# Second layer's dense pass reordered, its queries and values loaded sooner, and the first attention's keys queued behind its queries

## The chip, the cores and the metric

The kernel runs on one core of one Trainium2 chip. The metric is the device time of one execution in microseconds; the median of three runs is 2421.66 (2420.82 to 2422.63). The engines are TensorE (PE; weight loads PEld), VectorE (DVE), ScalarE (ACT), GpSimd (POOL) and SyncE (SP), which here only issues DMAs.

## What is computed

Two transformer layers with a layer norm behind each part, on 2048 tokens of width 512, in float32:

```
x = layernorm(x + causal_attention(x))        # 16 heads of 32, rotary on half of each head
x = layernorm(x + experts(x))                 # 8 experts, top 2, and a shared one
x = layernorm(x + attention(x))               # one head of 512, q and k with bias and rotary
x = layernorm(x + gated_mlp(x, 2 of 4 kept))
```

Second layer's attention: `q = rope((x Wq + bq) * scale)`, `k = rope(x Wk + bk)`, `v = x Wv + bv`, `softmax(q kT) v Wo`. Rotary: `[x1, x2] -> [x1 cos - x2 sin, x2 cos + x1 sin]` with x1 and x2 the halves of a head of 128.

## The kernel before

Each engine has a program of its own, written out in order; semaphores order the engines among each other. Every product is made of three passes (`mm3`): each operand is split into a high part (ACT's copy to a reduced type) and a low part (DVE subtracts the high part).

**First attention** (`layer0_attention`). The work is cut into 16 items n = (chunk c of 512 queries, group g of 4 heads). A planner (`attention0_plan`) writes one list `order`, that PE, ACT, DVE and POOL all follow: "unit" (a block of scores for the row maxima), "turn" (maxima transposed), "scores", "av", "den". SP loads queries into 3 slots and keys into 8 slots (an item of chunk c uses c + 1 slots) and stores and reloads the row of maxima ("m": store, wait, load). Its list `work` is sorted by a place in `order`: the place at which the slot comes free, or at which the turn three items before stands (`soon`). A load of queries or keys is three DMAs of 256 KB (L528 keys, L534 queries). PE waits at the first unit of an item for its queries, then for its keys (L705 is the units' matmul, L726 and L731 that of the scores).

**Second layer's dense pass** (`layer1_attention`). Four chunks c of 512 tokens, four tiles k of 128 in each. Four pairs p of pieces in a chunk: queries 0 and 1, keys 0 and 1, keys 2 and 3, queries 2 and 3. PE makes for a chunk eight pieces i of 512 x 512 (`piece`, a ring of four banks `qk`: piece i waits for ACT's and DVE's reading of piece i-4), transposes (`turn`, L1844) and values (`value`) of tiles. For a pair p:

- ACT `out(i)` (L1557) copies a piece with its bias to `qkf`; DVE `turning` (L1711) makes bias and sine product `across`; POOL `cosines` (L1486) multiplies both halves of `qkf` with the cosines in one instruction of 1024.
- DVE (L1716, L1717) subtracts and adds: `turned`. ACT `high` (L1571) makes the high half, DVE `low` (L1726) the low half. For queries SP stores both to `q_dram` (L1437), keys stay in SBUF.

Beside it the tiles of the next chunk are prepared: POOL gathers two rows of experts' results per token (`gather`), DVE adds them to X and takes statistics (`stats`, L1678 to L791), ACT `root`, DVE `apply` (L1690, L1692), ACT `apply` (L1537) norm the tile; PE transposes it (tile k waits for DVE's `turn` of tile k-2), ACT and DVE `turn` (L1546, L1698) split it to `xch`, `xcl`. Values: ACT and DVE `value` (L1579, L1730) write `vhl`, of two buffers, SP `v_out` (L1426) stores it; ACT's `value(k)` waits until the store of tile k-2 has landed. SP's order in a chunk: the queries of pairs 0 and 3, the next chunk's tables `cs`, then four value tiles.

Behind the pass tile n = 0 of the attention has its scores already (`scores(0, b)` with `qf`); PE then runs `scores(n + 1, b)` (needs `load(n + 1)`, L1422) between the transposes of tile n (L1932), and the A·V product of tile n. The values are read back from `v_dram` as eight loads of 1 MB (L1461), high and low for each chunk; A·V of tile 0 waits for them quarter by quarter (`vload`). DVE `peak(0)`, ACT `exps(0)` (L1586) stand between scores and transposes.

## Time and profile before

| | |
|---|---|
| median of three runs | 2421.66 us |
| the profiled execution's own time | 2422.3 us |
| its span | 2420.5 us |
| PE busy | 2215.2 us, 92% |
| DVE, ACT, POOL busy | 1212.9, 746.1, 640.3 us |
| first attention | about 165 to 790 us |
| second layer's dense pass | about 1280 to 1462 us |
| second layer's attention behind it, then MLP | from 1475 us |

All times of rows are of one execution, in us from the start of its span; "ns" is written where meant. A timeline row says when an instruction started and how long it took; [x <- y] says how long the engine stood idle before it and whose semaphore ended that. PEclk is the clock that TensorE was granted, 1.00 for 2.4 GHz and 0.50 for 1.2 GHz.

### The profile page before, as it was taken

How to read it: one execution, taken by the hardware profiler on the slowest of the kernel's cores; microseconds unless marked ns; L12 is line 12 of the kernel's file. 1: busy time of each engine (PE TensorE's matmuls, PEld its weight loads, DVE VectorE, ACT ScalarE, POOL GpSimd, SP SyncE). 2: the span in 40 equal slices, each digit the busy share in tenths (PEclk: the TensorE clock that was granted, in tenths of full speed). 3: DMA queues.
4: the chain of work that ended last, by engine and by line, in shares of the span. 5: the costliest groups of instructions: out<-in, count | busy, mean ns of one | idle time of the engine just before them, and what ended most of it. 6: DMA issues, size and time to landing. Idle time of an engine off the chain costs nothing. (4 is left out here: it accounts for less than half of the span.)

```text
span 2420.5 us, 27398 instructions
## 1 busy us (share of the span) xinstructions
PE 2215.2 (92%) x10140; PEld 1521.5 (63%) x10140; DVE 1212.9 (50%) x2272; ACT 746.1 (31%) x1334; POOL 640.3 (26%) x434
## 2 busy tenths in 40 slices
PE   7977999999999679999988887999999999999996
PEld 5854555555553444444446776888887787878775
DVE  6864577776661543222237662322325555455656
ACT  3322455555556332111124331111113221121222
POOL 4342455564556105010023433000003021211200
PEclk9976799999999889999999998999999999999998
DMA  4564244443210524132234435000001010100001
GB/s 172 179 179 123 80 114 124 109 97 79 66 27 19 174 97 174 61 118 79 79 118 131 148 105 200 27 23 21 27 27 53 1 35 18 35 17 17 18 18 52
DMA packets 102058, 196.07 MB, mean 81 GB/s; under 512 B 10080, under 2 KB 27360, under 8 KB 100512
## 3 DMA queue, kind: packets, MB, share of 16 engines
q1 hardware_dynamic: 92832, 164.29, 22.6%
q0 software_dynamic: 8240, 27.01, 3.3%
q10 hardware_dynamic: 864, 3.15, 0.4%
q8 instruction: 77, 1.26, 0.2%
q14 instruction: 45, 0.37, 0.1%
HBM read 127.69 MB, written 66.72 MB: 80 GB/s over the span
## 5 line engine op out<-in xcount | busy, mean ns | idle before, releaser
L619 ACT ACTIVATE a_probs<-a_stb 128x512 f32<-128x512 f32 (+3 forms) x640 | 308.8, 535 | 283.4 <-PE a_stb L731 168.3
L590 POOL TENSOR_TENSOR a_probs<-a_probs 128x1024 f32<-128x1024 f32 (+3 forms) x160 | 281.5, 1773 | 289.6 <-PE a_avb L743 274.6
L645 DVE TENSOR_REDUCE a_mparts<-a_sbank 128x1 f32<-128x512 f32 x384 | 239.6, 683 | 100.0 <-PE a_sbank L705 99.8
L2049 POOL CAST m_wh<-wst 128x1024 fp32r<-128x1024 f32 x24 | 27.8, 1157 | 732.6 <-POOLq L1367 377.0
L56 PE MATMUL m_gu<-hi,m_wh 128*128 128x512 f32 x512 | 202.9, 396 | 14.5 <-DVE m_h L2115 13.1
L58 PE MATMUL m_gu<-hi,m_wl 128*128 128x512 f32 x512 | 202.0, 395 | 0.0
L57 PE MATMUL m_gu<-lo,m_wh 128*128 128x512 f32 x512 | 201.9, 394 | 0.0
L743 PE MATMUL a_avb<-a_probs,V 128*32 128x512 f32 (+3 forms) x1280 | 155.3, 558 | 0.7 <-ACT a_probs L619 0.7
L650 DVE CUSTOM_DVE_ANT_0 a_junk<-a_sbank,hidden 128x128 bf16<-128x128 f32 (+3 forms) x256 | 113.6, 488 | 83.5 <-PE a_sbank L705 81.7
L705 PE MATMUL a_sbank<-hi,q 96*128 96x512 f32 (+3 forms) x320 | 133.6, 447 | 23.7 <-PEq L152 12.1
L2115 DVE TENSOR_TENSOR m_h<-m_sg,m_gu 128x512 f32<-128x512 f32 x64 | 43.9, 686 | 208.5 <-ACT m_sg L2079 208.4
L705 PE MATMUL a_sbank<-lo,q 96*128 96x512 f32 (+3 forms) x320 | 120.0, 411 | 17.5 <-DMA q<-qk 11.1
L726 PE MATMUL a_stb<-q,hi 97*128 97x512 f32 (+3 forms) x320 | 133.1, 427 | 1.6 <-ACT a_probs L619 1.5
L1810 DVE TENSOR_TENSOR ptl<-q_tb,pth 128x512 fp32r<-128x512 f32 x64 | 44.1, 691 | 157.5 <-ACT pth L1661 157.5
L2079 ACT ACTIVATE m_sg<-m_gu 128x512 f32<-128x512 f32 x64 | 38.3, 598 | 273.2 <-PE m_gu L58 250.1
L726 PE MATMUL a_stb<-q,lo 97*128 97x512 f32 (+3 forms) x320 | 120.6, 389 | 1.6 <-ACT a_probs L619 1.1
L56 PEld LDWEIGHTS m_gu<-hi,m_wh 128*128 128x128 f32 x512 | 97.8, 191 | 37.8 <-DVE m_h L2115 15.6
L1661 ACT ACTIVATE pth<-q_tb 128x512 fp32r<-128x512 f32 x64 | 38.2, 598 | 254.5 <-PE q_tb L1932 254.5
L56 PE MATMUL q_qk<-hi,q 128*128 128x512 f32 x240 | 98.6, 411 | 13.4 <-DMA q<-q 13.4
L58 PEld LDWEIGHTS m_gu<-hi,m_wl 128*128 128x128 f32 x512 | 97.7, 191 | 20.6
L57 PEld LDWEIGHTS m_gu<-lo,m_wh 128*128 128x128 f32 x512 | 97.7, 191 | 20.4
L726 PEld LDWEIGHTS a_stb<-q,hi 97*128 97x128 f32 x320 | 62.6, 198 | 68.2 <-ACT a_probs L619 34.0
(263 smaller groups left out, 4727.1 us busy)
## 6 DMA issues: line engine op xcount, KB each, us to landing
qk<-v_hl SPq DMA_DIRECT2D x32, 512.0 KB, 2.9
hi<-qk SPq DMA_DIRECT2D x60, 256.0 KB, 4.8
lo<-qk SPq DMA_DIRECT2D x60, 256.0 KB, 5.9
q<-qk SPq DMA_DIRECT2D x48, 256.0 KB, 5.6
wst<-in_w_mlp SPq DMA_DIRECT2D x24, 512.0 KB, 3.5
xs<-a_zeros POOLq DMA_DIRECT2D x39, 256.0 KB, 2.5
w<-xs SPq DMA_DIRECT2D x39, 256.0 KB, 2.8
ys<-e_rows_b SPq DMA_DIRECT2D x39, 256.0 KB, 2.0
```

The source lines that it names most:

```text
L56: nc.tensor.matmul(out, wh, xh, start=start, stop=False, skip_group_check=True)
L57: nc.tensor.matmul(out, wh, xl, start=False, stop=False, skip_group_check=True)
L58: return nc.tensor.matmul(out, wl, xh, start=False, stop=stop, skip_group_check=True)
L590: nc.gpsimd.tensor_tensor(probs[:, i % PSLOTS, hs, w0:], probs[:, i % PSLOTS, hs, w0:], probs[:, (i + 1) % PSLOTS, hs, w0:], ALU.add)\
L619: nc.scalar.activation(probs[:, i % PSLOTS, h, w0:], stb[:, k % 3, w0:], ACT.Exp, scale=SCALE0)\
L645: nc.vector.reduce_max(to, sbank[:, b, :], AX).then_inc(s["unit_max"], 1)
L650: nc.vector.tensor_tensor_reduce(out=junk[:, k % 2, 0:w], in0=sbank[:, b, 0:w], in1=hidden[:, CH - w:CH], scale=1.0, scalar=BIG, op0=ALU.a ...
L705: nc.tensor.matmul(bank[:, 0:w], qst[0:96, n % QSLOTS, h, t * P:(t + 1) * P], kst[at % KSLOTS][0:96, h, 0:w], start=True, stop=True)\
L726: last = nc.tensor.matmul(stb[:, k % 3, w0:], kst[slot_of[n, kt // TC] % KSLOTS][0:97, h, kt % TC * P:(kt % TC + 1) * P], qst[0:97, n % QS ...
L743: last = nc.tensor.matmul(avb[HD0 * h:HD0 * (h + 1), w0:], V[:, kt, g * P + h * HD0:g * P + (h + 1) * HD0], probs[:, i % PSLOTS, h, w0:], ...
L1810: nc.vector.tensor_tensor(ptl[:, 4 * g:4 * g + 4, :].rearrange("p a b -> p (a b)"), tb[:, (g + 1) % 2, :], f32(pth[:, 4 * g:4 * g + 4, :]) ...
L2115: tt(h[:, r, :], sg[:], gu[:, r % 2, 1, :], ALU.mult).then_inc(s["h_ok"], 1)
```

## The change

In the first attention a key load of item n is sorted no earlier than the query load of item n-1. In the dense pass DVE's `turning` is cut into `sines` and `sums`, between which statistics or transposed tiles can stand; POOL's cosines become one instruction of 512 for each half; on ACT and DVE some steps change places (DVE: `stats(n+2)` and `stats(n+3)` ahead of the sums, `apply(n+2)` ahead of `low(p)`, `turn(n)`, `turn(n+1)` ahead of the last sums, `value(n-2)` ahead of the last `low`). At its end SP loads the queries of tile 1 and three of the eight value loads right behind the last query store, ahead of the last two value stores.

```diff
--- before.py
+++ after.py
@@ -540,17 +540,18 @@
                 sp.dma_start(f32(qst[96:97, n % QSLOTS]).rearrange("o h n -> o (h n)"),
                              m_dram[n].rearrange("r q -> (r q)").unsqueeze(0)).then_inc(mrow[n % 2], 16)
 
-            work = []
+            work, queries = [], -1
             for n, (c, g) in enumerate(items):
                 soon = order.index(("turn", n - EARLY - 1)) if n > EARLY else -1
                 if n >= EARLY:
                     after = final[n - QSLOTS] if n >= QSLOTS else -1
-                    work.append((max(scored[after, 3] if after >= 0 else -1, soon), len(work), "q", n, 0, after))
+                    ahead, queries = queries, max(scored[after, 3] if after >= 0 else -1, soon)
+                    work.append((queries, len(work), "q", n, 0, after))
                 for j in range(c + 1):
                     at = slot_of[n, j]
                     after = last_use[loads[at - KSLOTS]] if at >= KSLOTS else -1
                     if at >= EARLY:
-                        work.append((max(scored[after, 3] if after >= 0 else -1, soon), len(work), "k", n, j, after))
+                        work.append((max(scored[after, 3] if after >= 0 else -1, soon, ahead), len(work), "k", n, j, after))
                 work.append((order.index(("turn", n)), len(work), "m", n, 0, 0))
             for _, _, what, n, j, after in sorted(work):
                 if what == "q":
@@ -1421,6 +1422,12 @@
                 for a in range(2):
                     sp.dma_start(f32(q[:, 1 - n % 2, a, :, :]), q_dram[a, :, :, n * P:(n + 1) * P]).then_inc(qload[n % 2], 16)
 
+            def values_in(c, half, dst):
+                ts = slice(c * TC, (c + 1) * TC)
+                for i in range(2):
+                    sp.wait_ge(vstore[i], 16 * (c + 1) * TC // 2)
+                sp.dma_start(f32(dst[:, ts, :]), v_dram[half, :, ts, :]).then_inc(vload[c], 16)
+
             def v_out(k):
                 sp.wait_ge(s["vl_ok"], k + 1)
                 sp.dma_start(v_dram[:, :, k, :].rearrange("a p n -> p a n"), f32(vhl[:, k % 2, :, :]))\
@@ -1437,10 +1444,15 @@
                         sp.dma_start(q_dram[a, :, j:j + 2, cols], f32(qhl[:, a, :, :])).then_inc(s["qstore"], 16)
                 if p % NP == NP - 1:
                     if c + 1 < NC:
-                        sp.wait_ge(s["cos_ok"], p + 1)
+                        sp.wait_ge(s["cos_ok"], 2 * p + 2)
                         sp.wait_ge(s["sin_ok"], 2 * p + 2)
                         sp.dma_start(cs[:], rope[:, :, (c + 1) * CH:(c + 2) * CH].rearrange("a p n -> p a n"))\
                             .then_inc(s["csload"], 16)
+                    else:
+                        load(1)
+                        for half, dst, early in ((0, vh, (0, 1)), (1, vl, (0,))):
+                            for i in early:
+                                values_in(i, half, dst)
                     for k in range(c * TC + 2, min(c * TC + TC + 2, NT)):
                         v_out(k)
                 elif p == NP:
@@ -1449,16 +1461,9 @@
                         sp.dma_start(f32(qf[:, a, :, :]), q_dram[a, :, :, 0:P]).then_inc(s["qfirst"], 16)
 
             sp.wait_ge(s["v_ok"], NT)
-            for c in range(NC):
-                if c == 1:
-                    sp.wait_ge(s["lo_ok"], NC * NP)
-                    sp.wait_ge(s["qstore"], 16 * NC * NP)
-                    load(1)
-                ts = slice(c * TC, (c + 1) * TC)
-                for i in range(2):
-                    sp.wait_ge(vstore[i], 16 * (c + 1) * TC // 2)
-                for a, dst in ((0, vh), (1, vl)):
-                    sp.dma_start(f32(dst[:, ts, :]), v_dram[a, :, ts, :]).then_inc(vload[c], 16)
+            for c, half, dst in ((1, 1, vl), (2, 0, vh), (2, 1, vl), (3, 0, vh), (3, 1, vl)):
+                values_in(c, half, dst)
+            sp.wait_ge(s["qstore"], 16 * NC * NP)
             for n in range(2, NT):
                 load(n)
             for i in range(2):
@@ -1478,13 +1483,14 @@
 
             def cosines(p):
                 c, which, j = pair(p)
-                pool.wait_ge(s["qkf_ok"], 2 * p + 2)
                 if p % NP == 0:
                     pool.wait_ge(s["csload"], 16 * (c + 1))
                 if p >= 2:
                     pool.wait_ge(s["lo_ok"], p - 1)
-                nc.gpsimd.tensor_tensor(turned[:, p % 2], qkf[:, p % 2], cs[:, 0, :].unsqueeze(1).broadcast_to([P, 2, CH]),
-                                        ALU.mult).then_inc(s["cos_ok"], 1)
+                for half in range(2):
+                    pool.wait_ge(s["qkf_ok"], 2 * p + half + 1)
+                    nc.gpsimd.tensor_tensor(turned[:, p % 2, half, :], qkf[:, p % 2, half, :], cs[:, 0, :], ALU.mult)\
+                        .then_inc(s["cos_ok"], 1)
 
             for k in range(TC):
                 gather(k)
@@ -1553,7 +1559,7 @@
                     act.wait_ge(s["consts"], 32)
                 act.wait_ge(s["qk_ok"], i + 1)
                 if p >= 2 and half == 0:
-                    act.wait_ge(s["cos_ok"], p - 1)
+                    act.wait_ge(s["cos_ok"], 2 * (p - 1))
                 nc.scalar.activation(qkf[:, p % 2, half, :], qk[:, i % 4, :], ACT.Identity,
                                      bias=bqk[:, which, j + half:j + half + 1]).then_inc(s["qkf_ok"], 1)
 
@@ -1581,7 +1587,7 @@
             def exps(n):
                 act.wait_ge(s["sbias_ok"], n + 1)
                 if n == 0:
-                    act.wait_ge(s["cos_ok"], NC * NP)
+                    act.wait_ge(s["cos_ok"], 2 * NC * NP)
                     act.wait_ge(s["sum_ok"], NC * NP)
                 nc.scalar.activation(pr[:], sc[:], ACT.Exp, bias=bias[:], scale=SCALE1, accum_out=rsum[:])\
                     .then_inc(s["exp_ok"], 1)
@@ -1634,19 +1640,20 @@
                 if c + 1 < NC:
                     apply(n + 2)
                 out(i + 6)
-                high(p + 2)
                 if c + 1 < NC:
                     root(n + 3)
+                high(p + 2)
                 out(i + 7)
                 if c + 1 < NC:
+                    apply(n + 3)
                     turn(n)
                     turn(n + 1)
-                high(p + 3)
-                if c + 1 < NC:
-                    apply(n + 3)
+                    value(n - 2)
+                    high(p + 3)
                 else:
+                    high(p + 3)
                     exps(0)
-                value(n - 2)
+                    value(n - 2)
                 value(n - 1)
                 if c + 1 < NC:
                     turn(n + 2)
@@ -1698,7 +1705,7 @@
                 tt(xcl[:, :, t * P:(t + 1) * P], tb[:, k % 2, :].rearrange("p (d t) -> p d t", d=ND),
                    f32(xch[:, :, t * P:(t + 1) * P]), ALU.subtract).then_inc(s["xl_ok"], 1)
 
-            def turning(p):
+            def sines(p):
                 c, which, j = pair(p)
                 if p % NP == 0:
                     dve.wait_ge(s["csload"], 16 * (c + 1))
@@ -1711,8 +1718,10 @@
                     nc.vector.scalar_tensor_tensor(across[:, half, :], qk[:, (2 * p + half) % 4, :],
                                                    bqk[:, which, j + half:j + half + 1], cs[:, 1, :], ALU.add, ALU.mult)\
                         .then_inc(s["sin_ok"], 1)
+
+            def sums(p):
                 dve.wait_ge(s["sin_ok"], 2 * p + 2)
-                dve.wait_ge(s["cos_ok"], p + 1)
+                dve.wait_ge(s["cos_ok"], 2 * p + 2)
                 tt(turned[:, p % 2, 0, :], turned[:, p % 2, 0, :], across[:, 1, :], ALU.subtract)
                 tt(turned[:, p % 2, 1, :], turned[:, p % 2, 1, :], across[:, 0, :], ALU.add).then_inc(s["sum_ok"], 1)
 
@@ -1774,36 +1783,41 @@
                     stats(n + 1)
                     apply(n)
                     apply(n + 1)
-                turning(p)
+                sines(p)
                 if c + 1 < NC:
                     stats(n + 2)
-                low(p)
-                turning(p + 1)
+                sums(p)
                 if c + 1 < NC:
                     apply(n + 2)
+                low(p)
+                sines(p + 1)
+                sums(p + 1)
                 low(p + 1)
-                turning(p + 2)
+                sines(p + 2)
                 if c + 1 < NC:
                     stats(n + 3)
-                low(p + 2)
-                turning(p + 3)
+                sums(p + 2)
                 if c + 1 < NC:
                     apply(n + 3)
-                low(p + 3)
+                low(p + 2)
+                sines(p + 3)
                 if c + 1 < NC:
                     turn(n)
                     turn(n + 1)
+                sums(p + 3)
+                if c + 1 < NC:
                     value(n - 2)
+                    low(p + 3)
                     value(n - 1)
                     turn(n + 2)
                     turn(n + 3)
                     value(n)
                     value(n + 1)
                 else:
+                    low(p + 3)
                     peak(0)
                     value(n - 2)
                     value(n - 1)
-
             for n in range(NT):
                 for g in range(4):
                     dve.wait_ge(s["ph_ok"], n * 4 + g + 1)
```

## Rows read from the trace of the kernel before

**Rows 1.** PE's table of waits: engine, line, awaited; us in total, times, longest.
```profile
PE a_sbank L705 <- DMA q<-qk: 18.9, 3, 11.1
...
PE q_tb L1844 <- DVE q_xcl L1698: 13.9, 3, 6.1
...
PE q_qk L56 <- DVE q_across L1711: 9.0, 3, 3.7
```

**Rows 2.** SP's timeline, first attention: start, length, line, operation, count of DMAs.
```profile
195.74 1.26 SPq L528 DMA_DIRECT2D hi<-qk  x3
...
198.47 2.15 SPq L534 DMA_DIRECT2D q<-qk  x3
...
224.62 1.25 SPq L534 DMA_DIRECT2D q<-qk  x3
...
258.61 1.25 SPq L534 DMA_DIRECT2D q<-qk  x3
```

**Rows 3.** PE's timeline, first attention: start, length, operation, [idle before <- released by].
```profile
195.77 0.28 PE L731 MATMUL a_stb<-maskr,identr 128*128 128x128 f32 x1
...
209.34 6.74 PE L705 MATMUL a_sbank<-lo,q 96*128 96x128 f32 x16 [11.08 <-DMA q<-qk]
...
232.28 9.55 PE L705 MATMUL a_sbank<-hi,q 96*128 96x512 f32 x16 [5.53 <-DMA q<-qk]
...
264.87 0.96 PE L705 MATMUL a_sbank<-hi,q 96*128 96x512 f32 x3 [2.34 <-DMA q<-qk]
...
276.07 0.39 PE L726 MATMUL a_stb<-q,hi 97*128 97x512 f32 x1
```

**Rows 4.** Two microseconds of the windows view: busy time and count by engine, PEclk, DMA.
```profile
256.00:258.00 2.00, 2.00 (x13) 0.31 (x5) 0.00 (x0) 0.00 (x0) 0.73 (x1) 0.50 0.00 0
```

**Rows 5.** PE's timeline, first chunk of the dense pass.
```profile
1304.89 0.47 PE L56 MATMUL q_qk<-q_xch,q_wh 128*128 128x512 f32 x1 [2.62 <-DVE q_across L1711]
...
1323.06 1.94 PE L1844 MATMUL q_tb<-ident,X 128*128 128x128 f32 x8 [6.10 <-DVE q_xcl L1698]
```

**Rows 6.** DVE's timeline, first chunk of the dense pass.
```profile
1294.58 1.41 DVE L1711 SCALAR_TENSOR_TENSOR q_across<-q_qk,bqk,q_cs 128x512 f32<-128x512 f32 x2 [1.84 <-ACT q_qkf L1557]
...
1298.79 0.68 DVE L1678 TENSOR_TENSOR X<-X,rows 128x512 f32<-128x512 f32 x1
...
1301.14 2.95 DVE L1726 TENSOR_TENSOR qhl<-q_turned,qhl 128x1024 fp32r<-128x1024 f32 x1
```

**Rows 7.** ACT's timeline, dense pass.
```profile
1301.26 0.30 ACT L795 ACTIVATE norm_std<-norm_mv,norm_eps 128x1 f32<-128x1 f32 x1 [0.71 <-DVE norm_mv L791]
...
1320.00 1.06 ACT L1571 ACTIVATE qhl<-q_turned 128x1024 fp32r<-128x1024 f32 x1 [2.97 <-DVE q_turned L1717]
...
1330.33 0.60 ACT L1579 ACTIVATE vhl<-q_vb 128x512 fp32r<-128x512 f32 x1 [4.69 <-DMA v<-vhl]
...
1459.80 1.98 ACT L1586 ACTIVATE pr<-q_qk,bias 128x2048 f32<-128x2048 f32 x1 [3.52 <-DVE bias L1736]
```

**Rows 8.** POOL's timeline, first chunk of the dense pass.
```profile
1300.63 2.38 POOL L1486 TENSOR_TENSOR q_turned<-q_qkf,q_cs 128x1024 f32<-128x1024 f32 x1 [0.24 <-ACT q_qkf L1557]
```

**Rows 9.** SP's timeline, last chunk of the dense pass.
```profile
1434.88 22.88 SPq L1437 DMA_DIRECT2D q<-qhl  x4
```

**Rows 10.** The page's list of DMA issues: count, size each, median us to landing.
```profile
qk<-v_hl SPq DMA_DIRECT2D x32, 512.0 KB, 2.9
```

**Rows 11.** PE's timeline behind the dense pass: first scores of tile 1, first A·V.
```profile
1475.26 0.76 PE L56 MATMUL q_qk<-hi,q 128*128 128x512 f32 x1 [13.45 <-DMA q<-q]
...
1489.38 0.48 PE L56 MATMUL q_vb<-vh,pth 128*128 128x512 f32 x1
...
1497.67 0.39 PE L56 MATMUL q_vb<-vh,pth 128*128 128x512 f32 x1
```

**Rows 12.** Two microseconds of the windows view behind the pass; columns as in rows 4.
```profile
1476.00:1478.00 2.00, 2.00 (x7) 1.51 (x6) 0.00 (x0) 0.00 (x0) 0.00 (x0) 0.50 0.99 410
```

**Rows 13.** Groups by form on POOL: count, busy us, mean ns, idle before.
```profile
L590 POOL TENSOR_TENSOR a_probs<-a_probs 128x512 f32<-128x512 f32 x24 | 30.7, 1281 | 37.8 <-PE a_avb L743 34.5 <-ACT a_probs L619 3.3
```

## The prediction

> **What bounds the kernel now.** The table of engines on the page gives TensorE (PE) 92% of the span, so a change can only give back time in which PE stands still or runs at its lower clock. I therefore read PE's table of waits first: three of its entries belong to the parts that the change touches, 18.9 us for query loads in the first attention, and in the second layer's dense pass 13.9 us before transposes that wait for `xcl` and 9.0 us before projections that wait for the sines [rows 1]; a fourth, 13.45 us for the queries of tile 1, is one stall [rows 11]. They make 55.2 us, the most that standing still offers here. Then I read the same places as timelines: SP and PE in the first attention [rows 2, 3], PE in the dense pass [rows 5], and beside it the three engines that feed it [rows 6 to 8].
>
> **Part 1, first attention: keys behind queries.** Unit matmuls of item 3 need queries q3, those of item 4 need q4, those of item 5 need q5. Before, SP issues the keys of item 5 (two slots, six DMAs, from 195.74) ahead of q3 (198.47). PE starts on q3 at 209.34, after 11.08 us; that is 10.87 us from the issue. q5, with no keys ahead of it, takes 264.87 − 258.61 = 6.26 us. q4 has one slot of keys ahead and takes 232.28 − 224.62 = 7.66 us [rows 2, 3]. So each slot ahead costs some 1.4 to 2.3 us.
> The new sort key puts the keys of item n behind the queries of item n−1. Worked through the planner's order by hand, SP then does m2, q3, keys of 4, m3, q4, keys of 5, q5, keys of 6, m4; from item 8 on nothing moves. q3 waits for the last scores of step 3 (195.77 + 0.28 = 196.05) [rows 3], is issued at 196.1, lands at 196.1 + 6.3 to 6.6 = 202.4 to 202.7. PE had nothing from 209.34 − 11.08 = 198.26, so the stall is 4.1 to 4.4 instead of 11.08: **6.8 us**. q4 is released by its own scores as before; without its slot of keys its load takes 6.26 to 6.6: **1.2 us**. q5 stays at 2.34 [rows 3]: nothing. Together 8.0 us.
> The price is at m4: the row of maxima of item 4 (a store, a wait for it, a load) now stands behind q5 and two slots of keys. At the 10.87 − 6.26 = 4.6 us which two slots cost, twice at most 9.2, it lands between 271 and 276; the first scores that use it run at 276.07 [rows 3]. Nothing, but with a thin margin.
> The clock: PE is granted 1.2 GHz at 256 to 258, as in all stretches from 230, that is, ever since the second stall, and 2.4 GHz soon after 258 [rows 4]. Whether a stall of 4.3 us leads to the same as one of 5.53 no row here shows; I take the same loss as before. If it came back earlier or later, the 16 us from 242 to 258, at half speed, would give back up to 8 or cost a few more.
>
> **Part 2, end of the dense pass: queries and values sooner.** Before, SP waits for the last values, then loads the first 2 MB of values, then the queries of tile 1; PE starts on them at 1475.26 after 13.45 us [rows 11]. Now SP issues them after the last query store, which is out at 1434.88 + 22.88 = 1457.8 [rows 9]. Behind that 0.5 MB store, the 0.5 MB of queries land at about 1462.5. PE cannot start before the first exponentials, 1459.80 + 1.98 = 1461.8 and the read of their sum [rows 7], so it starts at 1462.4: 12.9 us earlier. Behind the long stall the granted clock was 1.2 GHz until 1478 [rows 12]; these 2.7 us at half speed cost 1.3 and go with the stall: 14.1 in all, if nothing else is late. The first A·V then starts at 1489.38 − 14.1 = 1475.3 [rows 11].
> What is late next: values. The queues moved 410 GB/s in this stretch [rows 12], so a load of 1 MB takes 2.56 us. From 1457.9: store and queries (1 MB), three early value loads (3 MB), the two value stores (1 MB), three loads (3 MB), two more (2 MB). That is 10 MB, 25.6 us, 1483.5; with 1.5 us for the landing (a store of 0.5 MB lands 2.9 us after its issue [rows 10], 1.3 of them transfer), 1485. A·V wants its last quarter 8.3 us after its start (1497.67 − 1489.38 [rows 11]), at 1483.6. So 1.5 to 2 us are given back, and the queries of tile 2 (0.5 MB more) come at about 1486.5, before the 1488 at which they are wanted. Net **12.2 us**. The moved loads pass two value stores on SP: these wait now behind 3.5 MB, 9 us, and only the last quarter of values waits for them, already counted. `load(1)` has no wait of its own, and the stored tiles that the early loads read were written long before.
>
> **Part 3, the dense pass itself.** In a chunk PE stalls twice: 2.62 us before piece 6 for the sines of pair 1, 6.10 us before the transposes of tiles n+2, n+3 for `xcl` [rows 5]; chunks 1 and 2 repeat both, with which they add up to the 9.0 and 13.9 of [rows 1], and chunk 3 has neither. The new order puts `turn(n)` and `turn(n+1)` on VectorE ahead of the last `sums`, `value(n-2)` and `low`. That shortens the 6 us stall for certain, to about 3. But PE's stalls aren't what sets the chunk's period. Follow the loop: ScalarE (ACT) does the last `high` at 1320.00; SP stores it, its low half, loads the tables and stores two values; only when the first of these has landed does ACT do `value(n)` at 1330.33 [rows 7]; statistics and norms of the next chunk follow, then its sines. This ring runs through every chunk, and the change leaves SP's order in it as it was. So I ask whether the time from first sine to last `high` shrinks. Before: 1294.58 to 1320.00 [rows 6, 7], 25.4 us.
> After, with durations from these rows: sines end at 1296.0. Statistics come next (2.35 us, from 1298.79, where the sums end, to 1301.14 [rows 6]); cosines of the second half run on GpSimd (POOL) from 1295.8 to 1297.1 (a 512-wide operation has 1281 ns, so two halves cost 2.56 for 2.38 [rows 8, 13]). DVE's first addition reads two tensors in SBUF, as `low` does. `low` started at 1301.14 with POOL busy since 1300.63 and took 2.95 us, ending 1.1 us after POOL did [rows 6, 8]; an addition of half its size took 0.68 [rows 6], so it was held for some 1.7. So statistics end at 1299.2 and the sums at 1300.5 (before 1298.8). `high` 1.06 follows on ACT, then `out`, half as wide, and `root` 0.30 [rows 7], and here is the new wait: `apply(n+2)` now stands ahead of `low(p)` on DVE and waits for that root, until 1302.5; behind it are `low(p)`, whose start is delayed by some 1 us against its `high`, the sines of pair 1 and so piece 6. `low` ends at 1304.6, the sines start there instead of at about 1304.0: the stall before piece 6 grows to 3.3. Pair 1 gains 0.2 from halves, pair 2 has statistics ahead of its sums (sums at 1313.4 for 1311.4), pair 3 has two turns ahead. Carried on in this way the last `high` comes at 1322.0, 2.0 us later, and the period of the ring grows by 1.6 in each chunk. Against that PE enters each chunk less far behind the ring. The same recurrence run on the old order gives stalls of 2.7 and 6.3 and a pass that ends within 1.5 us of the profile's; on the new one PE reaches the last chunk 0.4 us later and ends the pass **0.3 us** later. With POOL never blocking DVE it would be 2.5 earlier; with halves at 1.35 us, 2.2 later; I keep −3 to +3.
> The Trainium skill has the rule for this ("SBUF — State Buffer", section "Who interferes with whom"): of GpSimd and a DVE instruction with two SBUF inputs the one that issues second blocks for the whole of the other. The 2.95 us row [rows 6] agrees; by it the new overlaps cost, without it the pass would be the 2.5 us shorter just given.
>
> **Sum.** 2420.5 − 8.0 − 12.2 + 0.3 = 2400.6 us of span. The profiled run took 2422.3, 1.8 more than its span; the median 2421.66 is 1.2 above the span, so 2401.8.
>
> **Rivals.**
> A, the pass opens up: ring and sines get faster by 2 to 3 us a chunk because overlaps with POOL fall luckily. For it: 22.9 us of PE stalls in the pass [rows 1]. Against it: the wait for `root` and the unchanged stores. 5 to 10 us more: 2392 to 2397. 12%.
> B, values late: the queue serves stores and loads together worse than 410 GB/s, or SP is held at an issue, so that the A·V of tile 0 stalls at several quarters. 4 to 7 us given back: 2406 to 2409. 12%.
> C, the clock in the first attention returns sooner after a shorter stall: up to 8 us, 2394 to 2399; 10%.
> D, slower: the ring. POOL has now eight short cosine instructions in a chunk; if each of the twelve two-SBUF instructions of DVE in a chunk were held by 0.6 us and the held `low` then held POOL, a chunk would grow by 7 us. From 20.5 / 3 = 6.8 us a chunk on it eats both gains: about 2427. 4%.
> E, it doesn't do what it says: q3 is held at its own wait or m4 is late by as much as q3 gains, and the early loads meet a full queue. Within 0.2%, 2418 to 2424. 4%.
> My forecast has 58%: 2398.5 to 2405.
>
> **Chances.** 0.2% is 4.8 us, about what a measurement of this kernel can tell from no change. Faster 58 + 12 + 12 + 10 = 92%, same 4%, slower 4%. The range for 8 in 10 takes in the forecast, B, C and most of A: 2393 to 2409.
>
> **What would show it.** PE's stall before q3's units near 4 us, before q4's near 4.3, before q5's unchanged; 2.4 GHz granted again only some 10 us or more after each. In the pass a stall before piece 6 of over 3 us, one before the transposes of 3 or less, new ones before piece 4 of chunks 1 and 2 of about 3; ACT's `value(n)` again released by a DMA. At its end no stall over 1 us before scores of tile 1, one of up to 2 us inside the first A·V, none later. A pass that ends 5 us sooner or later than 1461.8 less 8, or a clock that returns at once in the first attention, makes the prediction wrong.

## The result, and the profile after

| | before | changed |
|---|---|---|
| median | 2421.24 us (2420.48 to 2422.63, 4 runs) | 2405.89 us (2405.18 to 2408.62, 4 runs) |
| ratio | | 0.9939, 95% interval 0.9927 to 0.9952 |
| span of the profiled execution | 2420.5 us | 2404.6 us |

The changed kernel is 15.4 us faster (0.6%); 2401.8 was predicted. The span can be cut at places that every kernel here has, on PE's timeline: the end of the third stall for queries in the first attention, the first projection of the dense pass, the end of its last value product, the transposes of the attention's next tile behind the first A·V, and the end.

| stretch of PE's time, us | before | changed | difference | predicted |
|---|---|---|---|---|
| start to end of the third query stall | 264.87 | 257.15 | −7.7 | −8.0 |
| from there to the first projection | 1020.92 | 1021.96 | +1.0 | 0 |
| dense pass | 175.86 | 180.81 | +5.0 | +0.3 |
| behind the pass, to the next tile's transposes | 41.47 | 29.30 | −12.2 | −12.2 |
| from there to the end | 917.4 | 915.4 | −2.0 | 0 |

These are differences of one profile each, and such stretches vary by themselves. In the fourteen profiles of this study the second stretch, in which PE's instructions were the same in all, took 1020.9 to 1028.9 us, and the last one 915.1 to 918.2. The first stretch ended at 264.87, 264.40 and 261.22 us in the three kernels with the old order of loads and at 254.4 to 257.8 in eleven with the new one. The −2.0 at the end is such a difference too: two kernels that keep the old loads at the end of the pass took 915.4 and 915.3 us there. The pass is the term that was wrong.

First attention, PE's timeline of the changed kernel (rows 3 answer to it) and then SP's (rows 2); columns as there:

```profile
206.53 1.90 PE L706 MATMUL a_sbank<-lo,q 96*128 96x128 f32 x6 [4.90 <-DMA q<-qk]
...
228.25 2.38 PE L706 MATMUL a_sbank<-hi,q 96*128 96x512 f32 x4 [4.15 <-DMA q<-qk]
...
257.15 1.65 PE L706 MATMUL a_sbank<-hi,q 96*128 96x512 f32 x3 [3.35 <-DMA q<-qk]
```

```profile
199.50 1.26 SPq L534 DMA_DIRECT2D q<-qk  x3
...
221.97 1.26 SPq L534 DMA_DIRECT2D q<-qk  x3
...
250.40 1.25 SPq L534 DMA_DIRECT2D q<-qk  x3
```

Each load of queries now takes 6.3 to 7.0 us from issue to PE's start on them (10.9, 7.7 and 6.3 before). Two windows show the clock, PEclk being the number ahead of the last two:

```profile
196.00:198.00 2.00, 2.00 (x14) 0.79 (x17) 0.00 (x0) 0.55 (x2) 0.41 (x1) 0.50 0.02 4
...
244.00:246.00 2.00, 1.24 (x9) 0.95 (x7) 1.97 (x9) 0.99 (x4) 1.92 (x2) 1.00 0.00 0
```

PE was still at 1.2 GHz at 196 to 198 and so came to its first stall 3.4 us later than before (206.53 − 4.90 = 201.6 against 198.3); but it had 2.4 GHz again by 244, where before it had 1.2 GHz until 258 [rows 4]. The late start is a matter of this execution: in the thirteen other profiles, new order or old, PE had 2.4 GHz at 196 to 198 and its first stall began at 196.9 to 199.1. The early return is not: with the new order it came at 240 to 244 in all eleven profiles, with the old one at 247, 260 and 270.

The dense pass, first chunk. PE (rows 5 answer to it), DVE (rows 6), POOL (rows 8) and ACT (rows 7):

```profile
1300.48 0.77 PE L56 MATMUL q_qk<-q_xch,q_wh 128*128 128x512 f32 x1 [4.89 <-DVE q_across L1718]
...
1315.59 1.23 PE L1858 MATMUL q_tb<-ident,X 128*128 128x128 f32 x8 [0.97 <-DVE q_xcl L1705]
...
1317.99 0.47 PE L56 MATMUL q_vb<-q_wh,q_xch 128*128 128x512 f32 x1 [1.18 <-DVE vhl L1739]
```

```profile
1287.90 1.41 DVE L1718 SCALAR_TENSOR_TENSOR q_across<-q_qk,bqk,q_cs 128x512 f32<-128x512 f32 x2 [1.84 <-ACT q_qkf L1563]
1289.22 1.76 DVE L1685 TENSOR_TENSOR X<-X,rows 128x512 f32<-128x512 f32 x1
...
1292.65 2.34 DVE L1725 TENSOR_TENSOR q_turned<-q_turned,q_across 128x512 f32<-128x512 f32 x1
...
1297.47 0.16 DVE L1697 RECIPROCAL norm_rstd<-norm_std 128x1 f32<-128x1 f32 x1 [1.88 <-ACT norm_std L796]
...
1299.60 1.40 DVE L1718 SCALAR_TENSOR_TENSOR q_across<-q_qk,bqk,q_cs 128x512 f32<-128x512 f32 x2
```

```profile
1287.89 2.54 POOL L1492 TENSOR_TENSOR q_turned<-q_qkf,q_cs 128x512 f32<-128x512 f32 x2 [3.48 <-ACT q_qkf L1563]
...
1292.16 0.95 POOL L1480 DMA_INDIRECT rows<-ys,slot_b  x1 [0.30 <-issue]
1293.12 1.30 POOL L1492 TENSOR_TENSOR q_turned<-q_qkf,q_cs 128x512 f32<-128x512 f32 x1
```

```profile
1317.28 1.06 ACT L1577 ACTIVATE qhl<-q_turned 128x1024 fp32r<-128x1024 f32 x1 [2.27 <-DVE q_turned L1726]
...
1327.18 0.60 ACT L1585 ACTIVATE vhl<-q_vb 128x512 fp32r<-128x512 f32 x1 [7.39 <-DMA v<-vhl]
```

From the first sine (1287.90) to the last `high` (1317.28) are 29.4 us, before 25.4 [rows 6, 7]. ACT still waits (7.39 us) for the landing of a store ahead of `value(n)`. The turns' stall fell from 6.10 to 0.97, but the one before piece 6 grew from 2.62 to 4.89 [rows 5], and in PE's table of waits, which rows 1 show for the kernel before, the sines now take the larger part:

```profile
PE q_qk L56 <- DVE q_across L1718: 19.8, 5, 6.0
...
PE q_tb L1858 <- DVE q_xcl L1705: 2.9, 3, 1.6
```

Behind the pass, PE's timeline (rows 11), then SP's end (rows 9):

```profile
1459.92 0.39 PE L56 MATMUL q_qk<-hi,q 128*128 128x512 f32 x1
...
1472.59 0.47 PE L56 MATMUL q_vb<-vh,pth 128*128 128x512 f32 x1
...
1483.66 0.47 PE L56 MATMUL q_vb<-vh,pth 128*128 128x512 f32 x1 [2.15 <-DMA vl<-v]
```

```profile
1450.47 2.75 SPq L1444 DMA_DIRECT2D q<-qhl  x2
...
1460.49 1.34 SPq L1433 DMA_DIRECT2D v<-vhl  x2
...
1471.06 0.32 SPq L1429 DMA_DIRECT2D vh<-v  x1
```

The 13.45 us ahead of the scores of tile 1 are gone, with 2.15 us before the last quarter of A·V in their place.

### The profile page after: what moved, and what is told of

It reads as the page before. It is cut to its first block and busy times, and to the rows that moved or that the text cites. A ratio compares the mean times of both kernels' runs of the same rounds, so it can differ in the third digit from the quotient of the medians.

```text
span 2404.6 us, 27418 instructions
## 1 busy us (share of the span) xinstructions
PE 2212.6 (92%) x10140; PEld 1517.3 (63%) x10140; DVE 1221.2 (51%) x2272; ACT 745.6 (31%) x1334; POOL 643.0 (27%) x450
## 5 line engine op out<-in xcount | busy, mean ns | idle before, releaser
L2063 POOL CAST m_wh<-wst 128x1024 fp32r<-128x1024 f32 x24 | 27.4, 1140 | 721.4 <-POOLq L1368 367.5
L727 PEld LDWEIGHTS a_stb<-q,lo 97*128 97x128 f32 x320 | 61.2, 192 | 69.6 <-issue 47.9
```

The source lines that it names most:

```text
L727: last = nc.tensor.matmul(stb[:, k % 3, w0:], kst[slot_of[n, kt // TC] % KSLOTS][0:97, h, kt % TC * P:(kt % TC + 1) * P], qst[0:97, n % QS ...
```

## The experiments

In what follows "pass" is PE's time from the first projection to the end of the last value product, and "behind the pass" the time from there to the next tile's transposes. They tell more than whole times: one execution's whole time carries the unchanged stretches' own spread of some 8 us. The pass has a spread as well: with the same instructions it took 175.9, 176.9, 175.9 and 176.2 us in four profiles and 180.8 and 179.8 in two, so a difference of 1 us between two passes says nothing. The "chain" is the time from the first sine to the last `high` of the first chunk; it repeats to 0.1 us (25.4 to 25.5 in the four, 29.4 in the two).

### The three parts, alone and left out

Each was built from the two kernels by taking the diff's parts as they are: the planner's sort key (first attention); the loads of queries and values (end of the pass); everything that ACT, DVE and POOL do in the dense pass.

The sort key alone:

```diff
+            work, queries = [], -1
...
+                    ahead, queries = queries, max(scored[after, 3] if after >= 0 else -1, soon)
+                    work.append((queries, len(work), "q", n, 0, after))
...
-                        work.append((max(scored[after, 3] if after >= 0 else -1, soon), len(work), "k", n, j, after))
+                        work.append((max(scored[after, 3] if after >= 0 else -1, soon, ahead), len(work), "k", n, j, after))
```

> The kernel before with the first part alone: in the first attention the keys queue behind the queries of the item before. Theory (each part stands alone): the profiled stall before item 3's queries falls from 11.1 to about 4.5 us, before item 4's from 5.5 to 4.2, item 5's stays between 2.3 and 3.4; the time falls by 7 us, by 3 to 10 according to how long the clock stays at 1.2 GHz behind the stalls; the dense pass takes 176 us as before. Rival (the parts need one another, or the clock gives the gain and not the loads): stalls shrink but the time moves by less than 3 us.

Measured: 2415.33 us (10 runs), ratio 0.9971 (0.9959 to 0.9983), 7 us. Stalls 4.92, 4.48 and 3.17 us. This is the theory's 7 us, with the second stall a little over its 4.2.

The loads alone:

```diff
+                    else:
+                        load(1)
+                        for half, dst, early in ((0, vh, (0, 1)), (1, vl, (0,))):
+                            for i in early:
+                                values_in(i, half, dst)
...
-            for c in range(NC):
+            for c, half, dst in ((1, 1, vl), (2, 0, vh), (2, 1, vl), (3, 0, vh), (3, 1, vl)):
+                values_in(c, half, dst)
```

> The kernel before with the second part alone: queries of tile 1 and three value loads behind the last query store. Theory: the 13.45 us stall goes, one stall of about 2 us before the last quarter of values comes, 12 to 14 us less, about 2408 us. Rival (early loads delay the value stores and cost more inside the first A.V): stalls there of 5 us or more, 8 us less or smaller.

Measured: 2411.30 us (4 runs), ratio 0.9953 (0.9935 to 0.9972). Behind the pass 33.1 us instead of 41.5: 8.3 gained, not 12.2. The whole time gained 11.4 us by the ratio, with an interval of 6.8 to 15.7, so it can't tell the two apart. Neither theory nor rival came out: the stalls before the last two quarters of values were 1.50 and 2.12 us, not 5.

The pass alone:

```diff
-                turning(p)
+                sines(p)
                 ...
+                sums(p)
                 if c + 1 < NC:
                     apply(n + 2)
+                low(p)
...
-                pool.wait_ge(s["qkf_ok"], 2 * p + 2)
...
+                for half in range(2):
+                    pool.wait_ge(s["qkf_ok"], 2 * p + half + 1)
```

> The changed kernel with parts one and two undone: only the dense pass's orders and the cosines by halves. Ring theory (the ring from sines over the last high, the value store's landing and the statistics sets a chunk's time, and the new order makes it longer): the pass from its first projection to its last value takes 181 us instead of 176, the kernel is 4 to 6 us slower than before, about 2426, a chunk from one value(n) released by its store to the next takes about 49 us instead of 46 to 47. Rival (the pass by itself is as quick or quicker, the 5 us come from what the early loads or the shifted clock do to it): within 1.5 us of before or faster.

Measured: 2429.42 us (7 runs), ratio 1.0026 (1.0012 to 1.0039), 6 us: slower, as the ring theory had it, and the rival is out. Pass 179.8 us (before 175.9; the theory said 181), the stall before piece 6 again 4.90, 49.8 and 46.9 us from one `value(n)` to the next (before 46.7 and 44.8).

The first two together, the pass as before:

> The changed kernel with the dense pass's orders and whole cosines of before: parts one and two together. Ring theory: the two gains add up, 19 to 21 us less than before, about 2401, and 4 to 6 us less than the changed kernel. Rival (the pass's new order is needed for the early loads, since it ends the last chunk's query stores sooner): no faster than the changed kernel, 2404 or more.

Measured: 2405.85 us (7 runs), ratio 0.9937 (0.9919 to 0.9955), not to be told from the changed kernel's 0.9939: the rival came out, in the whole time. Its pass took 176.2 us, 4.7 less than the changed kernel's, and it gave back nearly all of it: 33.9 us behind the pass instead of 29.3. Its PE timeline there:

```profile
1455.45 0.47 PE L56 MATMUL q_qk<-hi,q 128*128 128x512 f32 x1 [0.63 <-DMA q<-q]
...
1476.32 0.47 PE L56 MATMUL q_vb<-vh,pth 128*128 128x512 f32 x1 [1.99 <-DMA vl<-v]
...
1481.42 0.77 PE L56 MATMUL q_vb<-vh,pth 128*128 128x512 f32 x1 [2.10 <-DMA vl<-v]
```

and a window of it behind the second of these stalls, with PEclk 0.66 where the changed kernel had 1.00 all the way behind the pass:

```profile
1482.00:1486.00 4.00, 4.00 (x13) 3.17 (x12) 0.00 (x0) 0.00 (x0) 0.00 (x0) 0.66 0.15 38
```

So the pass part cost 4.7 us in the pass and paid about as much behind it.

### Which step of the pass cost the 4 to 5 us

`apply(n+2)` back behind the second pair's sums, so that DVE doesn't wait for ACT's `root`:

```diff
                 sums(p)
-                if c + 1 < NC:
-                    apply(n + 2)
                 low(p)
                 sines(p + 1)
                 sums(p + 1)
+                if c + 1 < NC:
+                    apply(n + 2)
```

> The changed kernel, with VectorE's two norms' apply (of the next chunk's tiles) back behind the second pair's sums, where the kernel before had it; nothing else. Theory: in the changed kernel VectorE stood 1.88 us in each of three chunks for ScalarE's root ahead of the first pair's low half, and with the apply's own additions that put the second pair's sines 11.7 us behind the first pair's; with the apply back these sines come 2 us or more earlier, the last high of the chunk 1 us earlier, and the pass (first projection to last value on TensorE) takes 177.5 to 179 us instead of 180.8. Rival 1, the holds by GpSimd's multiplies are all of the loss and the wait costs nothing: 180 to 181.5. Rival 2, the apply only moves to a worse place: over 181.5.

Measured: pass 180.2 us, chain 28.5; rival 1 came out for the pass, though the last `high` came 0.9 us sooner as the theory had it. The 1.88 us wait did vanish and the second pair's sines came 1.8 us sooner, but their sums then ran beside POOL's products:

```profile
1301.66 1.40 DVE L1718 SCALAR_TENSOR_TENSOR q_across<-q_qk,bqk,q_cs 128x512 f32<-128x512 f32 x2
1303.10 1.55 DVE L1725 TENSOR_TENSOR q_turned<-q_turned,q_across 128x512 f32<-128x512 f32 x1
```

(The 2412.2 us of its whole time is one execution in which the second stretch took 1026.5 us, and the last one 2.8 us more than in the changed kernel.)

The cosines' product in one instruction:

```diff
-                for half in range(2):
-                    pool.wait_ge(s["qkf_ok"], 2 * p + half + 1)
-                    nc.gpsimd.tensor_tensor(turned[:, p % 2, half, :], ...).then_inc(s["cos_ok"], 1)
+                pool.wait_ge(s["qkf_ok"], 2 * p + 2)
+                nc.gpsimd.tensor_tensor(turned[:, p % 2], ...).then_inc(s["cos_ok"], 2)
```

> The changed kernel, with GpSimd's cosine multiply of a pair in one instruction again (it waits for both halves of the pair) instead of two. Theory: VectorE's addition L1725, whose mean was 2.3 us where GpSimd's first multiply was queued behind a gather, and L1685, 1.76 us, are held by the halves; with one multiply at least one of them falls to its free length (about 1.2), and the pass takes 178 to 179.5 us instead of 180.8. Rival, the hold only moves to the next addition of VectorE, since the same bytes go through GpSimd: 180.3 to 181.5 us, with another line at over 2 us. If the halves were a gain (the high half of a pair could start sooner), the pass would take over 181.5 us.

Measured: 2407.79 us (one execution), pass 179.6 us, chain 28.6. The pass lies 0.1 us over the theory's range, but the changed kernel's pass, built alone, took 179.8: it can't tell the theory from the rival. The chain can: 0.8 us shorter. The first sum (L1725; L1724 here) fell to 0.69 as the theory expected, but the first addition of the statistics rose from 1.76 to 2.22 and the first `low` from 1.88 to 3.02, as the rival had it: the hold moved, and little was left over. And behind the pass it took 33.3 us, about as in the two kernels above that also have one product (33.1 and 33.9). The last chunk tells a part of why. ACT's highs of its four pairs, in the changed kernel and then here:

```profile
1431.25 1.06 ACT L1577 ACTIVATE qhl<-q_turned 128x1024 fp32r<-128x1024 f32 x1 [0.36 <-DVE q_turned L1726]
1436.41 1.06 ACT L1577 ACTIVATE hi<-q_turned 128x1024 fp32r<-128x1024 f32 x1
1441.85 1.06 ACT L1577 ACTIVATE hi<-q_turned 128x1024 fp32r<-128x1024 f32 x1
1449.38 1.06 ACT L1577 ACTIVATE qhl<-q_turned 128x1024 fp32r<-128x1024 f32 x1 [4.89 <-DVE q_turned L1726]
```

```profile
1429.30 1.06 ACT L1576 ACTIVATE qhl<-q_turned 128x1024 fp32r<-128x1024 f32 x1 [1.28 <-DVE q_turned L1725]
1435.31 1.06 ACT L1576 ACTIVATE hi<-q_turned 128x1024 fp32r<-128x1024 f32 x1 [1.84 <-DVE q_turned L1725]
1441.32 1.06 ACT L1576 ACTIVATE hi<-q_turned 128x1024 fp32r<-128x1024 f32 x1 [2.41 <-DVE q_turned L1725]
1449.43 1.06 ACT L1576 ACTIVATE qhl<-q_turned 128x1024 fp32r<-128x1024 f32 x1 [6.47 <-DVE q_turned L1725]
```

They follow at 5.16, 5.44 and 7.53 us with halves and at 6.01, 6.01 and 8.11 with one product. PE's time from the last chunk's first sines to the end of the pass is the same (32.7 us), so the last `high` starts 10.5 us ahead of the pass's end with halves and 7.6 us ahead without. Behind it stand the last query stores, the queries of tile 1 and all values: they come 2.9 us sooner against PE. Of this PE gets some 2 us: its stalls behind the pass add up to 4.5 us in this kernel (4.3 and 4.7 in the other two with one product) and to 2.4 in the changed one.

The other 1.9 of the 4.0 us are the clock. All three kernels with one product had 1.2 GHz for some 3.4 us behind their last stall. This is not due to the one product alone: of the eight profiles with halves and the early loads, three had it too, behind a last stall of 2.1 us, as here in the kernel with the statistics alone moved back, which follows further below:

```profile
1480.00:1482.00 2.00, 2.00 (x6) 1.58 (x5) 0.00 (x0) 0.00 (x0) 0.00 (x0) 0.50 0.10 30
```

They took 30.5 to 31.2 us behind the pass, the four with 2.4 GHz throughout and the last `high` 10.5 us ahead 28.8 to 29.4. The eighth, the first kernel under "The ring", kept 2.4 GHz, but its last `high` is only 8.1 us ahead; it stood still for 4.0 us and took 31.2. That fits the stalls' part. Why the clock fell in some and not in others is not shown.

The statistics of tiles n+2 and n+3 behind the sums, where they stood before, with `root(n+3)` behind the third `high`:

```diff
                 sines(p)
-                if c + 1 < NC:
-                    stats(n + 2)
                 sums(p)
+                if c + 1 < NC:
+                    stats(n + 2)
...
-                if c + 1 < NC:
-                    root(n + 3)
                 high(p + 2)
+                if c + 1 < NC:
+                    root(n + 3)
```

> The changed kernel, with VectorE's statistics of the next chunk's tiles 2 and 3 behind the sums instead of ahead of them, and ScalarE's root of the fourth tile behind the third pair's high half. Theory (the wait for root and the holds are the loss, the place of the statistics is not): 180 to 182 us for the pass, against 180.8; the hold of L1725 goes away or gets smaller, since the sums start sooner than GpSimd's multiply, but the root comes later and the wait for it grows from 1.9 to 3 us or more. Rival, the statistics ahead of the sums are what delays the pairs: 178 to 179.5 us.

Measured: pass 170.9 us, chain 24.7, one execution of 2397.81 us: below both ranges; the rival named the right thing and asked for too little. DVE and then POOL:

```profile
1287.78 1.41 DVE L1718 SCALAR_TENSOR_TENSOR q_across<-q_qk,bqk,q_cs 128x512 f32<-128x512 f32 x2 [1.84 <-ACT q_qkf L1563]
1290.43 0.69 DVE L1725 TENSOR_TENSOR q_turned<-q_turned,q_across 128x512 f32<-128x512 f32 x1 [1.23 <-POOL q_turned L1492]
...
1291.64 0.69 DVE L1685 TENSOR_TENSOR X<-X,rows 128x512 f32<-128x512 f32 x1
...
1294.43 0.16 DVE L1697 RECIPROCAL norm_rstd<-norm_std 128x1 f32<-128x1 f32 x1 [0.36 <-ACT norm_std L796]
...
1296.79 1.40 DVE L1718 SCALAR_TENSOR_TENSOR q_across<-q_qk,bqk,q_cs 128x512 f32<-128x512 f32 x2
```

```profile
1287.78 2.54 POOL L1492 TENSOR_TENSOR q_turned<-q_qkf,q_cs 128x512 f32<-128x512 f32 x2 [3.48 <-ACT q_qkf L1563]
1290.47 1.51 POOL L1477 DMA_INDIRECT rows<-ys,slot_a  x1
```

DVE stands still for 1.23 us, until POOL's second product is done, and then adds at full speed: L1725 starts 2.65 us behind the sines' start, where in the changed kernel it started 4.75 us behind it and ran 2.34 instead of 0.69. The idle time isn't what makes the difference. The wait for `root` shrinks from 1.88 to 0.36 us, since DVE now does the statistics while ACT does `high` and `out`, where it stood still before; together DVE stands still for 1.6 us here and for 1.9 there. What is gone are holds beside POOL's products: 1.08 us of the statistics' first addition and 1.65 of L1725, against 0.23 more of `low`. That gives the 2.7 us by which the second pair's sines follow sooner (9.0 us behind the first for 11.7). In the third pair another 1.65 us of hold and 0.4 of idle time go, and that is the chain, 24.7 for 29.4. The place of the statistics costs by what it makes run side by side.

The statistics alone moved back (`root(n+3)` left ahead of the third `high`):

> The changed kernel, with the statistics of the next chunk's tiles 2 and 3 behind the sums on VectorE; ScalarE's root of the fourth tile stays ahead of the third pair's high half (the kernel with both moved took 170.9 us for the pass, against 180.8 with neither). Theory: the place of the statistics is the whole gain, by 1.2 us of waiting for the cosines' product exchanged for 3.4 us of statistics, and by the additions that ran beside GpSimd; but ScalarE's third high now stands behind the statistics, some 2.5 us later, of which 0.5 to 2 us a chunk reach the last high: pass 172 to 176 us. Rival, moving the root was what gained: 179 to 182 us. Second rival, the third high has slack: 170.5 to 171.5 us.

Measured: 2403.13 us (one execution), pass 173.6 us, chain 25.4, as the theory had it. So of the 9.9 us (each figure good to about 1 us), 7.3 are the place of the statistics, and 2.6 the third `high`, which must not stand behind a root whose statistics are now later.

Statistics, root and `apply` all back:

> Statistics and the fourth root behind, as in the kernel whose pass took 170.9 us, and also the apply of the third tile back behind the second pair's sums, as in the kernel before. Theory: with the statistics behind the sums the wait for the root was only 0.36 us, and the low half that follows would start while GpSimd multiplies the next pair (it ran 2.11 us instead of 1.2), so that a start 0.7 us sooner is lost to a longer hold: 170.5 to 171.7 us, no gain from the apply's place. Rival, the wait for the root and the apply's own 0.3 us are on the chain: 169 to 170.2 us, with the second pair's sines 8.2 to 8.5 us behind the first pair's instead of 9.0.

Measured: 2396.27 us (one execution), pass 170.4 us, chain 24.7. The first `low` ran 2.81 us beside POOL instead of 2.11: the place of `apply` is worth nothing (170.4 against 170.9), nor was it where the statistics stood ahead (180.2 against 180.8).

### The ring

`value(n)` and `value(n+1)` of ACT and DVE behind the roots and statistics of the next chunk:

```diff
                 if c + 1 < NC:
                     root(n)
                     root(n + 1)
+                if c > 0:
+                    value(n - TC)
+                    value(n - TC + 1)
+                if c + 1 < NC:
                     apply(n)
                     apply(n + 1)
...
                     turn(n + 3)
-                    value(n)
-                    value(n + 1)
```

> The changed kernel, with the split of a chunk's last two value tiles (on ScalarE and VectorE) moved from ahead of the next chunk's roots and statistics to behind them. In the changed kernel ScalarE stood 7.4, 8.1 and 6.5 us in the three turns for the landing of a store that frees the split's buffer, and all of the next chunk stood behind it. Theory of the ring (this wait sets the chunk's period): taking it off the path gives back at least 2 and up to 3.5 us a turn, the pass takes 171 to 176 us instead of 180.8, TensorE's stalls inside of the pass fall from some 27 to under 18 us; whole kernel 2397 to 2402 us if the values for the first probabilities land as much sooner. Rival, VectorE's own work and GpSimd's holds set the period and the landing is waited for by an engine that has slack: 179.5 to 181.5 us, kernel 2404 to 2407. Third case, the pass is shorter but the last values land hardly sooner, as in the kernel with the old pass and both other parts: pass 171 to 176, kernel 2402 to 2405.

Measured: 2400.70 us (4 runs), ratio 0.9907 (0.9890 to 0.9923), pass 172.1 us with an unchanged chain of 29.4. ACT now does two roots where it stood still before, and hardly waits for the store:

```profile
1325.70 0.29 ACT L796 ACTIVATE norm_std<-norm_mv,norm_eps 128x1 f32<-128x1 f32 x1 [3.97 <-DVE norm_mv L792]
1328.02 0.30 ACT L796 ACTIVATE norm_std<-norm_mv,norm_eps 128x1 f32<-128x1 f32 x1 [2.02 <-DVE norm_mv L792]
1329.11 0.60 ACT L1585 ACTIVATE vhl<-q_vb 128x512 fp32r<-128x512 f32 x1 [0.80 <-DMA v<-vhl]
```

From chunk to chunk the first sines follow at 44.7, 46.4 and 40.1 us instead of 49.1, 49.8 and 40.4. So the 8.7 us come from two turns of the ring, 4.4 and 3.5 us: the landing of that store did set the period, as the prediction said. In the third turn there are no roots to put ahead, and ACT stands as long as before:

```profile
1418.42 0.60 ACT L1585 ACTIVATE vhl<-q_vb 128x512 fp32r<-128x512 f32 x1 [7.10 <-DMA v<-vhl]
```

Both edits together (statistics and root back, values behind the roots):

> The two edits that shortened the pass together: statistics of tiles 2 and 3 and the fourth root behind (170.9 us alone), and the split of a chunk's last two value tiles behind the next chunk's roots and statistics (172.1 us alone), from 180.8. Theory: they act on different links of one chain (first sine to last high: 24.7 us instead of 29.4; and the wait of 7 to 8 us for the store's landing), so their gains add but for where TensorE or another link becomes the limit: pass 162 to 166 us, whole kernel 2389 to 2396 us, with TensorE's stalls in the pass under 11 us. Rival, either alone already reaches the next limit (VectorE's own work of a chunk): pass 168 to 171 us, kernel 2396 to 2400. Third case, the pass is as short as by the theory but the values of the last chunks land late: stalls of 4 us or more in the first tile's product with the values, kernel 2393 to 2398.

Measured: 2389.90 us (4 runs, 2383.04 to 2392.52), ratio 0.9861 (0.9840 to 0.9881): 0.8% below the changed kernel's ratio of 0.9939 and the lowest of all. Pass 160.0 us, 20.8 less than the changed kernel, more than 9.9 and 8.7 together (the theory said 162 to 166); behind it 30.5. PE's waits for the sines:

```profile
PE q_qk L56 <- DVE q_across L1720: 8.3, 3, 3.0
```

The same with one cosine product in the first three chunks and halves in the last alone:

```diff
+                if c + 1 < NC:
+                    pool.wait_ge(s["qkf_ok"], 2 * p + 2)
+                    nc.gpsimd.tensor_tensor(turned[:, p % 2], ...).then_inc(s["cos_ok"], 2)
+                    return
                 for half in range(2):
```

> The kernel with both edits (pass 160.0 us, from the end of the pass to the next tile's transposes 30.5 us), with the cosines' product in one instruction a pair in the first three chunks and in two halves only in the last. In the last chunk the highs followed one another at 5.44 us with halves and at 6.01 us with one product, and the last query stores were issued 9.5 us ahead of the pass's end with halves and 6.5 to 6.6 us ahead without; in the three kernels without halves the stretch behind the pass took 33.1 to 33.9 us. Theory, the halves are worth their place in the last chunk alone: 30.0 to 31.0 us behind the pass as in the kernel with halves throughout, pass 158.5 to 160.5 us (the holds of VectorE's additions in the chunks before were 1.2 us of the pass in the changed kernel, and most of them went with the statistics' place), whole kernel 2387 to 2391 us. Rival 1, the halves of the earlier chunks decide what is late at the end: 33 us or more behind the pass. Rival 2, the halves let each pair of every chunk through sooner: pass over 161 us.

Measured: 2392.47 us (4 runs), ratio 0.9874 (0.9858 to 0.9891); pass 167.1 us, chain 26.5, behind the pass 31.2. Half of the theory held, but for 0.2 us: the stretch behind the pass needs halves only in the last chunk. The other half fell to rival 2: with the statistics behind, halves are worth 7 us of the pass. The whole times of the two kernels can't be told apart by their intervals; the passes can.

## Why the prediction was right, and where it wasn't

**The number.** 2405.9 lies in the range for 8 in 10, 2393 to 2409, but 0.9 us above the forecast's own, 2398.5 to 2405, next to rival B's 2406 to 2409, whose mechanism wasn't there. And of the prediction's own signs of being wrong one came true: the pass was to end at 1461.8 less 8, give or take 5 us, and ended at 1459.9, 6.1 us late. The sum missed by 4.1 us, the pass alone by 4.7; the stretches that were taken as unchanged (+1.0 and −2.0) gave a part of it back, which is luck. The forecast is right in its mechanisms and wrong in the size of one term. Of its other signs in the pass most came as said, the new stalls before piece 4 with 3.35 us in the second chunk but only 1.17 in the third, where both were to be about 3.

**First attention.** Right in sum (−7.7 for −8.0), less so in its terms, and with 3.7 us between three profiles of the old order the closeness is luck too. Stalls of 4.90 and 4.15 us came for 4.1 to 4.4 and 4.3; the queries took 7.0 us from issue instead of 6.3 to 6.6 and were issued 3.4 us later, since PE still ran at 1.2 GHz at 196 to 198 in this execution. "The same loss as before" was wrong for the clock behind the second stall: in all profiles with the new order 2.4 GHz came back sooner. Rival C's gain thus came in part, and was cut: with PE sooner at item 5 the third stall grew from 2.34 to 3.35. `m4` with its thin margin never made a stall.

**End of the pass.** −12.2 for −12.2. The scores of tile 1 start when the pass ends; the stalls ahead of the last two quarters of values were 0.24 and 2.15 us for 1.5 to 2 in all; the last value stores landed 10.6 us after SP issued the first of them, for the 9 us of queue reckoned. But the sum hid two conditions. In the kernel with these loads and one cosine product, 3.9 us of the 12.2 are missing: the working took the last query store's time from the kernel before and never said that halves bring it forward against PE's own end. And it took the clock as 2.4 GHz throughout, which three of the eight profiles with the same loads and halves did not have; they gained 10.3 to 11.0 us. That the term came out to the tenth is luck.

**Dense pass.** The mechanism named (a ring through the landing of the value store, whose chunk grows as the time from first sine to last `high` grows) was right; the value edit shows it. Its size was off, +5.0 for +0.3. The step that failed is "so statistics end at 1299.2 and the sums at 1300.5". Counted from the first sine that is 5.9 us to the end of the sums; it was 7.7. The hold of the statistics' first addition was there about as reckoned (1.76 us, 1.1 held). Missing was a second hold of 1.65 us: L1725 met the next pair's product on POOL. Everything behind was late by that: sines of pair 1 11.7 us behind the first for 10.0, last `high` 29.4 for 27.4, and two periods of the ring 49.9 and 47.6 us, 3.2 and 2.8 more than before where 1.6 was reckoned. It happened in the first pair of each of the three chunks, and in the third pair (L1725 at 1308.25, 2.33 us) of the first two; in the third chunk another addition was held there, for 1.66 us.

A second error is one of weight. The working set the statistics ahead of the sums against other small gains and called the pass neutral. The runs show it as two large terms of opposite sign: the place of the statistics, with the root that follows them, costs 9.9 us, and the rest of the new order gains 4.9 (175.9 to 170.9). No rival stood for "one of these moves is bad by itself", though the row of 0.68 us for an addition beside one of 2.95 [rows 6] had the price in it.

**Rivals.** A (the pass opens up) was wrong for this kernel but was there for the taking, in the two kernels that undo one move or hide the landing. B (values late) did not come with halves, and did, by some 2 us of stalls, in the three kernels without them. D's mechanism is the one at work, with four of DVE's instructions held in a chunk, by 0.7 to 1.65 us each, not twelve; its sign holds for the pass part alone (+0.26%). E is out.

Open: the two edits' gains add to more than their sum, 20.8 against 18.6 us. By the distances of the chunks' first sines the excess is 1.0 us; another 1.7 us stand in the last chunk, where the kernel with the statistics behind took 34.3 us from its first sines to the end of the pass and the one with both edits 32.6. Both are near the spread, and their cause wasn't tried; nor was what decides when the clock falls, in the first attention and behind the pass.

## What to carry to other kernels

Idle time of an engine that waits for a partner is not free to fill. Here work of 2.4 us put into a wait of 1.2 us sat on the chain with the rest, and it set additions beside the partner's products: each one that was held cost 1.1 to 1.65 us, where the idle time came out about even (1.6 us in the one order, 1.9 in the other). So look first at which two-input instructions a new order sets beside GpSimd's, and then at the idle time. When a change moves several steps, price each alone against the chain, since a sum near zero can be two large terms; and when the next stage waits for a transfer, count its start from the producer's last result, not from the end of the stage. Where a buffer is freed by a DMA's landing in every turn of a loop, put work that doesn't need the buffer between.

## What the chip showed that was not expected

A DVE addition with both inputs in SBUF can be held by a POOL product that starts after it. L1725 starts at 1292.65, 0.47 us ahead of POOL's product at 1293.12, and ends at 1294.99, 0.57 us behind the product's end at 1294.42; with POOL not multiplying it takes 0.69. The product stood directly behind a gather on POOL's queue (1292.16, 0.95 us), but gathers alone don't hold such an addition: L1688 ran its 0.69 us at 1291.02 wholly inside the gather from 1290.59 to 1291.85, and in the kernel with the statistics behind L1685 did at 1291.64 beside the gather that began at 1290.47. By the Trainium skill ("SBUF — State Buffer", section "Who interferes with whom") the one that issues first has the shared pair and the other waits; by the starts in these rows it is the other way round, and the measurement decides, as far as a row's start stands for the issue. The same order of starts came with 2.33 us at 1308.25 too. Why the later one wins is not shown.
